# A graph-attention layer with layer norm: units of four source blocks for two heads in place of units of two source blocks for four heads, and the sums of a group taken out of PSUM by another engine

## The reference

```
Wh    = (x @ W.T) as [4 heads, 8192, 32]
e     = leaky_relu(score_src[i] + score_dst[j], 0.2)      # per head
alpha = softmax over j of e where adj[i, j] != 0
h'    = alpha @ Wh                                        # per head
out   = layernorm(x + h')
```

## Time and profile before

| | |
|---|---|
| median of 3 runs | 1487.32 us (1482.68 to 1493.78) |
| profiled execution, its own time | 1484.16 us |
| its span from the first to the last instruction | 1482.3 us |
| mean granted TensorE clock | 0.954 of full |
| busy share of the span | ACT 90%, POOL 90%, DVE 88%, PE 81% |
| chain of work that ended last | PE 45%, POOL 19%, issue 14%, ACT 11%, DVE 5% |

### The profile page before, as it was taken

The page is one execution under the profiler, slowest core; times in us unless marked ns, Lnnn a source line. Parts: engine busy times, 40 slices in busy tenths (PEclk is TensorE's granted clock), DMA queues, the critical chain, the costliest instruction groups (busy, mean ns, idle before and its releaser), DMA issues.

```text
span 1482.3 us, 77436 instructions
## 1 busy us (share of the span) xinstructions
PE 1204.4 (81%) x35173; PEld 1177.2 (79%) x35173; DVE 1307.4 (88%) x1422; ACT 1333.5 (90%) x1456; POOL 1328.0 (90%) x1371
## 2 busy tenths in 40 slices
PE   7047679898888889888897989889887989888985
PEld 7036669897888889788897989888887879888984
DVE  6966669899898999999798999989999889989995
ACT  2799999999999999999999999999999999999753
POOL 1788879999999999999999999999999999999854
PEclk9569989999999999999999999999999999999997
DMA  8203555657757675656746675666657665675740
GB/s 162 57 30 34 50 73 53 62 80 67 94 47 95 55 97 57 64 80 67 91 45 94 61 72 74 64 87 57 93 51 97 58 61 77 67 80 49 73 46 24
DMA packets 55842, 101.65 MB, mean 69 GB/s; under 512 B 5721, under 2 KB 18393, under 8 KB 55513
## 3 DMA queue, kind: packets, MB, share of 16 engines
q0 software_dynamic: 36864, 67.13, 52.0%
q1 hardware_dynamic: 18648, 29.56, 6.2%
HBM read 293.67 MB, written 4.33 MB: 201 GB/s over the span
## 4 chain that ended last, share of the span: by engine, by line
PE 45%; POOL 19%; issue 14%; ACT 11%; DVE 5%; POOLq 0%; DVEq 0%; ACTq 0%
PE bank L754 40%; POOL kept L341 14%; ACT kept L465 10%; PE bank L742 5%; DVE kept L630 3%; POOL edge L337 2%; DVE rest L638 1%; DVE shift L678 1%; POOL late L371 1%; POOL y L380 0%; ACT late L492 0%; POOL late L367 0%; POOL late L358 0%; POOL late L364 0%; POOL late L374 0%
## 5 line engine op out<-in xcount | busy, mean ns | idle before, releaser
L465 ACT ACTIVATE kept<-s_two,sd 128x1024 uint8<-128x1024 f32 (+1 forms) x1152 | 1196.5, 1116 | 87.0 <-DVE rest L638 50.1
L341 POOL TENSOR_SCALAR kept<-s_two,sd 128x1024 uint8<-128x1024 f32 (+1 forms) x896 | 967.8, 1091 | 37.0 <-DVE rest L638 19.6
L630 DVE TENSOR_TENSOR kept<-bank,kept 128x1024 int32<-128x1024 int32 x512 | 621.3, 1216 | 111.1 <-PE bank L742 79.1
L754 PE MATMUL bank<-G,kept 128*128 128x66 f16 x16384 | 600.9, 194 | 106.6 <-issue 57.9
L638 DVE TENSOR_TENSOR rest<-kept,bank 128x1024 int32<-128x1024 int32 x512 | 618.5, 1209 | 33.6 <-PE bank L754 33.4
L754 PEld LDWEIGHTS bank<-G,kept 128*128 128x128 fp8e4 x16384 | 544.4, 98 | 120.4 <-issue 64.4
L754 PE MATMUL bank<-F,rest 128*128 128x66 f16 x16384 | 595.5, 194 | 46.2 <-issue 45.7
L754 PEld LDWEIGHTS bank<-F,rest 128*128 128x128 fp8e4 x16384 | 555.4, 98 | 51.0 <-issue 50.7
L742 PE MATMUL bank<-identb,edge 128*128 128x128 bf16 x2048 | 201.9, 222 | 17.2 <-issue 9.0
L337 POOL DMA_DIRECT2D edge<-in_adj x256 | 151.5, 593 | 16.0 <-DMA kept<-in_x 16.0
L742 PEld LDWEIGHTS bank<-identb,edge 128*128 128x128 bf16 x2048 | 125.0, 98 | 24.1 <-issue 10.0
(11 more groups left out here) (77 smaller groups left out, 405.4 us busy)
## 6 DMA issues: line engine op xcount, KB each, us to landing
edge<-in_adj POOLq DMA_DIRECT2D x256, 256.0 KB, 5.3
s_two<-sT_scratch SPq DMA_DIRECT2D x30, 512.0 KB, 6.5
kept<-in_x SPq DMA_DIRECT2D x16, 256.0 KB, 6.5
y<-in_x SPq DMA_DIRECT2D x16, 256.0 KB, 7.5
out<-y SPq DMA_DIRECT2D x16, 256.0 KB, 7.2
s_two<-sT_scratch SPq DMA_DIRECT2D x2, 256.0 KB, 6.5
y<-sT_scratch SPq DMA_DIRECT2D x1, 256.0 KB, 3.7
late<-sT_scratch SPq DMA_DIRECT2D x1, 256.0 KB, 4.8
```

What stands on the lines that cost most here:

```text
L341: return nc.gpsimd.tensor_scalar(out, scores, STEEP, d_steep[:, j, h:h + 1], ALU.mult, ALU.add)
L465: return nc.scalar.activation(out, scores, ACT.Sigmoid, scale=STEEP, bias=d_steep[:, j, h:h + 1])
L630: nc.vector.tensor_tensor(kept[:, :, both(k, k)[0]], edgeT[k % NT], kept[:, :, both(k, k)[0]], ALU.bitwise_and).then_inc(step_set, 1)
L754: last = nc.tensor.matmul(acc[k][:, col:col + BC], matrices[h][:, b * P:(b + 1) * P, e], values[:, t * E + e, h].rearrange("p s c -> p (s ...
```

## The change

- The unit k becomes (quad of four source blocks, pair of heads): 16 quads for a group, and for each quad two units, one for each two heads. One AND, one XOR, 32 + 32 matmuls and four compare tiles for a unit, as before; the tiles of a unit are now its four source blocks. Four matmuls in a row, not two, add into the same sum.
- A quad's edges are eight transposes and fill a whole PSUM bank; three banks hold three quads, and PE transposes two quads ahead. DVE's order for a quad is AND, AND, XOR, XOR; PE's is AND matmuls twice, eight transposes, XOR matmuls twice.
- `kept` has three spare quads, which is six units; a compare for unit k waits for unit k - 6. `rest` has two buffers as before.
- DVE, not ACT, takes the sums out of PSUM (take_sums): for each bank an add of a pair of parts (a reduction for F; a scaling and an add for G). Banks 0 and 1 stand in DVE's queue ahead of the next group's first two ANDs, banks 2 to 4 between these ANDs and the XORs. PE closes banks 0 and 1 before its last transposes and XOR matmuls, and opens a bank when it first needs it.
- One ratio exp((slope - 1) * max(s + d_max, 0)) takes the place of the two row factors; the common factor cancels in the division. POOL's steps go from eight to four. After the last group DVE does these four itself.
- The shift goes from DVE (L678) to POOL (behind the inverse deviation); DVE gets a small negation of the mean. The closing steps have new places (CLOSING, FINISH, DEVIATION, SCALED), the edge loads of a chunk one unit earlier (EDGE_UNITS).
- The prologue loses some small instructions on the row factors.

```diff
-    EDGE_UNITS = (2, 3, 4, 5)
+    EDGE_UNITS = (1, 2, 3, 4)
+    CQ = CP // U
     RINGS = HEADS // 2
-    NS = 5
-    PLACES = PAIRS + NS
+    NS = 3
+    PLACES = QUADS + NS
     MIDDLE = PLACES // 2
     NL = 2
     NT = 3
     AHEAD = 2
-    WORDS = ROWS * E // 4
+    WORDS = ROWS * E // 4 * U
...
-        every = [(e, r) for r in range(RINGS) for e in range(E)]
+        every = [(u, e) for u in range(U) for e in range(E)]
...
-        edgeT = [t[:, 0:WORDS].bitcast(i32).unsqueeze(1).unsqueeze(1).to_broadcast([P, RINGS, 2, WORDS]) for t in edge_bank]
+        edgeT = [t[:, 0:WORDS].bitcast(i32).unsqueeze(1).to_broadcast([P, 2, WORDS]) for t in edge_bank]
...
+        def quad_and_ring(k):
+
+            return k // RINGS, k % RINGS
...
-        CLOSING = (4, 6, 8, 10, 12, 14, 18, 20)
-
-        SUMS, FINISH, DEVIATION, SCALED = 4, 16, 26, 30
+        CLOSING = (7, 9, 17, 19)
+
+        FINISH, DEVIATION, SCALED = 12, 28, 31
...
             def close(g, part):
 
-                top, low = sums_G[:, :, 0:HC], sums_F[:, :, 0:HC]
-
-                def per_row(v, width):
-                    return v.rearrange("p b h -> p (b h)").unsqueeze(2).to_broadcast([P, CHUNKS, width])
-
-                rows = slice(g * IB, (g + 1) * IB)
                 if part == 0:
-                    pool.wait_ge(acc_act, done((g + 2) * BANKS))
-                    nc.gpsimd.tensor_tensor(low, low, sums_F[:, :, HC:FC], ALU.add).then_inc(low_set, 1)
+                    pool.wait_ge(acc_taken, done((g + 2) * BANKS))
+                    nc.gpsimd.tensor_tensor(sum_F, sum_F, per_row(ratio[:, g * IB:(g + 1) * IB, :], HC), ALU.mult).then_inc(low_set, 1)
                 elif part == 1:
-                    nc.gpsimd.tensor_scalar(sums_G[:, :, HC:BC], sums_G[:, :, HC:BC], 1.0 / LOW, None, ALU.mult).then_inc(top_set, 1)
+                    pool.wait_ge(low_set, g + 1)
+                    nc.gpsimd.tensor_tensor(sum_G, sum_G, sum_F, ALU.add).then_inc(top_set, 1)
...
                 nc.gpsimd.tensor_tensor(rstd[:, :], mv[:, :, 1], half_t[:, :], ALU.pow).then_inc(rstd_set, 1)
+                pool.wait_ge(rstd_set, g + 1)
+                nc.gpsimd.tensor_tensor(shift[:, :], minus_mean[:, :], rstd[:, :], ALU.mult).then_inc(shift_set, 1)
...
-                    if k >= NS:
-                        pool.wait_ge(step_done, k - NS + 1)
-                        pool.wait_ge(rest_set, k - NS + 1)
+                    q, r = quad_and_ring(k)
+                    if q >= NS:
+                        pool.wait_ge(step_done, k - RINGS * NS + 1)
+                        pool.wait_ge(rest_set, k - RINGS * NS + 1)
...
-            for part in range(len(CLOSING)):
-                close(GROUPS - 1, part)
             inverse_deviation(GROUPS - 1)
...
-            def take_sums(g):
-
-                act.wait_ge(var_set, done(g))
-                for b in range(BANKS):
-                    n = sums_in(b) * BC
-                    act.wait_ge(acc_done, g * BANKS + b + 1)
-                    nc.scalar.copy(late[:, b * USED:b * USED + n], acc[b][:, 0:n]).then_inc(acc_act, 1)
...
             def take_step(k):
 
-                dve.wait_ge(transposed, k + 1)
+                q, r = quad_and_ring(k)
+                dve.wait_ge(transposed, q + 1)
                 dve.wait_ge(act_compared, k + 1)
                 dve.wait_ge(pool_compared, k + 1)
-                nc.vector.tensor_tensor(kept[:, :, both(k, k)[0]], edgeT[k % NT], kept[:, :, both(k, k)[0]], ALU.bitwise_and
+                nc.vector.tensor_tensor(kept[:, r, both(q, q)[0]], edgeT[q % NT], kept[:, r, both(q, q)[0]], ALU.bitwise_and
                                         ).then_inc(step_set, 1)
 
             def take_rest(k):
 
+                q, r = quad_and_ring(k)
                 dve.wait_ge(step_set, k + 1)
                 if k >= NL:
                     dve.wait_ge(rest_done, k - NL + 1)
-                nc.vector.tensor_tensor(rest[:, k % NL], kept[:, :, both(k, k)[0]], edgeT[k % NT], ALU.bitwise_xor
+                nc.vector.tensor_tensor(rest[:, k % NL], kept[:, r, both(q, q)[0]], edgeT[q % NT], ALU.bitwise_xor
                                         ).then_inc(rest_set, 1)
+
+            def take_sums(g, b):
+
+                dve.wait_ge(acc_done, g * BANKS + b + 1)
+                first, end = b * PER_BANK, b * PER_BANK + sums_in(b)
+                unit_of = acc[b][:, 0:(end - first) * BC].rearrange("p (k s c) -> p k s c", s=BP, c=HC)
+                n_G = max(0, min(end, CHUNKS) - first)
+                if end > CHUNKS:
+                    at = first + n_G - CHUNKS
+                    last = nc.vector.tensor_reduce(sum_F[:, at:end - CHUNKS], unit_of[:, n_G:].rearrange("p k s c -> p k c s"), AX.X, ALU.add)
+                if n_G > 0:
+                    nc.vector.tensor_scalar(sum_G[:, first:first + n_G], unit_of[:, 0:n_G, 1], 1.0 / LOW, None, ALU.mult).then_inc(small_taken, 1)
+                    dve.wait_ge(small_taken, g * BANKS_G + b + 1)
+                    last = nc.vector.tensor_tensor(sum_G[:, first:first + n_G], unit_of[:, 0:n_G, 0], sum_G[:, first:first + n_G], ALU.add)
+                last.then_inc(acc_taken, 1)
...
             for g in range(GROUPS):
                 closing = iter(()) if g == 0 else finish(g - 1)
-                for t in range(PAIRS):
-                    take_step(pair_no(g, t))
-                    if t > 0:
-                        take_rest(pair_no(g, t - 1))
-                    if t >= FINISH and t % 2 == 0:
+                for t in range(0, PAIRS, RINGS):
+                    k = pair_no(g, t)
+                    if t == 0 and g > 0:
+                        take_sums(g - 1, 0)
+                        take_sums(g - 1, 1)
+                    for r in range(RINGS):
+                        take_step(k + r)
+                    if t == 0 and g > 0:
+                        for b in range(2, BANKS):
+                            take_sums(g - 1, b)
+                    for r in range(RINGS):
+                        take_rest(k + r)
+                    if t >= FINISH:
                         next(closing, None)
-                take_rest(pair_no(g, PAIRS - 1))
                 for _ in closing:
                     pass
-            for _ in finish(GROUPS - 1):
+
+            g = GROUPS - 1
+            for b in range(BANKS):
+                take_sums(g, b)
+            dve.wait_ge(acc_taken, done((g + 2) * BANKS))
+            nc.vector.tensor_tensor(sum_F, sum_F, per_row(ratio[:, g * IB:(g + 1) * IB, :], HC), ALU.mult).then_inc(low_set, 1)
...
+            def transpose_edges(q):
+
+                c = q // CQ
+                if q % CQ == 0:
                     pe.wait_ge(edge_loaded[c % NC], 16 * IB * (c // NC + 1))
-                if k >= NT:
-                    pe.wait_ge(rest_set, k - NT + 1)
+                if q >= NT:
+                    pe.wait_ge(rest_set, RINGS * (q - NT + 1))
+                for u in range(U):
+                    at = (q % CQ * U + u) * P
+                    for b in range(IB):
+                        last = nc.tensor.transpose(edgeT16[q % NT][:, (u * IB + b) * P:(u * IB + b + 1) * P],
+                                                   edge16[:, c % NC, b, at:at + P], identb[:, :])
+                last.then_inc(transposed, 1)
...
+            def add_quad(t, matrices, values, first, opened):
+
+                q, r = quad_and_ring(t)
                 for b in range(IB):
-                    last = nc.tensor.transpose(edgeT16[k % NT][:, b * P:(b + 1) * P],
-                                               edge16[:, c % NC, b, k % CP * P:(k % CP + 1) * P], identb[:, :])
-                last.then_inc(transposed, 1)
-
-            def add_pair(t, matrices, values, first, before=None, after=None):
-
-                for c in range(CHUNKS):
-                    b, h = c // HEADS, c % HEADS
-                    k, col = place_of(first + c)
-                    if before is not None and (first + c) % PER_BANK == 0:
-                        before(k)
-                    for e in range(E):
-                        last = nc.tensor.matmul(acc[k][:, col:col + BC],
-                                                matrices[h][:, b * P:(b + 1) * P, e],
-                                                values[:, t * E + e, h].rearrange("p s c -> p (s c)"),
-                                                start=False, stop=False, skip_group_check=True)
-                    if after is not None and (first + c + 1 == SUMS_OF or (first + c + 1) % PER_BANK == 0):
-                        after(k)
+                    for n, matrix in enumerate(matrices):
+                        h = RINGS * r + n
+                        k, col = place_of(first + b * HEADS + h)
+                        opened(k)
+                        for u in range(U):
+                            for e in range(E):
+                                last = nc.tensor.matmul(acc[k][:, col:col + BC],
```

(59 more changed lines are left out.)

159 lines of the change are left out of this document (63 added, 96 removed).

## The result

The changed kernel takes **1416.0 us** (median of 4 runs, 1407.2 to 1420.2) against 1486.6 for the kernel before (1482.7 to 1493.8): ratio 0.9512, 95% interval 0.9452 to 0.9572. I forecast 1448, with a range of 1412 to 1488. The sign and the range held, the range by 4 us; the gain is 70.6 us where I worked out 36 to 39.

What follows compares the result with a forecast made beforehand. POOL's queue (83 us a group) and PE with holes and waits (83.8) bound the kernel; PE falls to 82.1, gaining 2.0 us 13 times (-28 with the start), ends bring -36 in all, from 1484.2 to 1448 us, range 1412 to 1488.

Steps and rivals of the forecast that it cites:

- Two bounds near 84 at once: In a repeating group of 84.1 us, POOL's queue needs 83 and PE with holes and waits 83.8; both must be relieved.
- sums: DVE taking a group's five PSUM banks of sums costs 3.4 us, bounds 2.9 and 4.5.
- The ends: Outside the 13 repeating stretches: -7.3 us up to the first normalise, -2.7 after the stretches.
- The idles at a group's start: PE, when caught up, idles 1.6 then 1.5 us while DVE takes sums before the next group's ANDs and XORs.
- the slower rival: Idles at a group's start total 3.4 us and drop PE's clock; PE needs 85.7 a group, 1502 us; chance 0.12.
- The dear sums: Rival: DVE's nine small sum instructions are held up like L678, 2.4 us each; DVE needs 96, about 1640 us; chance 0.05.
- its own need: PE's busy 72.8 us plus 7.8 of "issue" a group, 80.6, carried over to the changed kernel.
- issue: PE's idle time without waiting for a semaphore, holes in its instruction stream; 7.8 us a group, forecast to stay near that.
- my signs of being wrong: "Issue" depending on matmul grouping, a sums row over 0.7 us, or one undivided idle at a group's start.
- DVE's waits would only move from the AND to the XOR: Longer lookahead frees the AND, but two XOR buffers keep DVE waiting for PE, some 3 to 4 us a group.
- the one in which the holes are absorbed: Rival: six spare units and PE's catching up hide the holes; 79.2 us a group, 1407 us; chance 0.15.
- the last group at 79.5: Argument against absorbed holes: the last group, without full-size compares or sums to take, still takes 79.5 us on PE.

Runs made afterwards that it cites:

- experiment 3: `units_only` with its closing steps moved apart, six units between a DVE step and the POOL step waiting for it, DVE's shift two quads later: 1534.3 us (1.0299).
- experiment 7: Changed kernel with transposes one quad ahead instead of two, behind the first of two AND blocks: 1411.7 us (0.9481).
- (8): Changed kernel with the earlier order by unit on DVE and PE, AND of unit k then XOR of unit k - 1: 1435.2 us (0.9674).
- (2): Kernel before, pairs for four heads kept, with sums on DVE, one ratio, four closing steps, shift on POOL and the new places: 1473.8 us (0.9914).
- units_new_places: The kernel of experiment 3, new units with ACT's copies and closing steps moved apart: 1534.3 us (1.0299).
- experiments 10 to 12: Changed kernel, epsilon and negated mean on POOL; edge loads at units 0/2/4/6; at 1/3/5/7, transposes one quad ahead; all at unit 1: 1488.8, 1479.4, 1459.5 us.
- units_only: Kernel before with units of a quad and two heads, keeping ACT's copies, POOL's eight closing steps and shift on DVE: 1541.4 us (1.0366).

## Why the prediction was right, and where it was off

**What held.** Two bounds near 84 at once, POOL's queue and PE with its holes, and a change that must relieve both: neither half alone brings the gain. Engine by engine (forecast, measured): ACT 77.9, 77.0; POOL 78.3 with its waits, 76.1 busy and (24.7 + 4.1 + 12.0) / 13 = 3.1 of waits, of which those for places come from DVE's pace; DVE 78.4, 78.3; sums 3.4, (19.0 + 12.9 + 13.3) / 13 = 3.5. Shift on POOL, a product, took 0.20 us, not the 1.04 that I took from L384, a power of the same size. The ends came out at -7.3 and -3.4 against -7.3 and -2.7. The idles at a group's start are 0.7 and 0.9 us, not 1.6 and 1.5, and the clock did not fall behind them, so that the slower rival had nothing to stand on. The dear sums fell too: nine instructions that read PSUM took 0.33 to 0.51 us on the mean beside POOL's compares. What I had not costed is L663, an instruction that stayed: 0.17 us before, 1.23 now. I had looked for contention with POOL only in instructions with two SBUF inputs; L663 has one (experiment 3).

**The step that failed** is the one in which I gave PE "its own need" of 72.8 + 7.8 = 80.6 and carried it over, with "issue" to stay near 7.8. It fell to 4.3. With 72.3 of matmuls and 3.2 of waits for DVE's ANDs and XORs that makes 79.8 of the group's 80.0, and what DVE does without stops, 78.3, became the floor. The 82.1 of the forecast contains the missing 2.1 us, 13 times. That "issue" might depend on how the matmuls are grouped stood among my signs of being wrong; its size did change, though no run shows that the grouping is what changed it. The second half of the same step, that DVE's waits would only move from the AND to the XOR at 3 to 4 us a group, follows it: 1.4 were measured, all at the XOR, as I had put the place; experiment 7 shows that the longer lookahead indeed buys nothing. These waits, at the AND and the XOR, are there in every kernel here that has holes of 7.8 us and over beside a full DVE (6.0, 5.6, 6.1, 4.8, 4.1), and small where the holes are about 4 (1.4, 1.3, 1.3). Of the rivals, the one in which the holes are absorbed (79.2 a group, 1407 us) came nearer than the forecast, and I gave it 0.15. The range held because I had drawn its lower end out to 1412 to take in half of that rival; 1416 lies 4 us inside it, and there is luck in that. My argument against it, the last group at 79.5, was again PE's busy time plus holes taken for a constant.

**Open.** What in the change shrank the holes is narrowed, not settled. It isn't the lookahead (7) nor the order by two (8), nor the sums (2): `units_new_places`, with ACT's copies, has holes of (48.0 + 4.2) / 13 = 4.0 too. What is left is the unit itself with its six spare units, and where the four loads of edges fall: the change moved them from units 2 to 5 to units 1 to 4, which I had not costed at all, and experiments 10 to 12 show that their place alone is worth 4 to 7 us a group. The unit by itself is not enough, since these three kernels have it and holes of 9.4 to 10.5. No run gave the pairs of before the loads of the change, or the change the loads of before. Nor do the runs say why loads every 2.8 us disturb PE's refills less in the change than loads every 5 or four at once, or than the loads of the kernel before.

## What to carry to other kernels

Idle time marked "issue" on PE is not a property of PE's program alone: look at what else the DMA engines carry when its instruction stream is refilled, and time a few places for the large loads. Some small DVE instructions with their data in SBUF (here TENSOR_SCALAR and those with two inputs) can take over ten times their length beside a POOL that never pauses; take the wait out of POOL's queue and it may come back in DVE's. A change with two halves that each remove one of two equal bounds is judged only as a whole.

## What was unexpected of the hardware

A 128 x 16 TENSOR_SCALAR of DVE took 5.4 us on the mean beside back-to-back compares on POOL, and 0.17 to 0.34 in the kernels where POOL waited for it in all or half of the groups (`units_only`, the change, the kernel before); those with a PSUM input took 0.33 to 0.51 throughout. PE's stream of 16.4 KB refills cost 0.33 us a group with no edges' loads. With them it cost 4.1 to 10.5 us in four kernels with the same bytes and the same work on every engine, which differ in when the loads were issued (and one of them in the lookahead, which made no difference in experiment 7).
